# The output projection of a macaron block: as a stage of its own, or as the end of the last head's part

## The reference

```python
x = x + 0.5 * ffn(layernorm(x))          # 512 -> 4096 (gate, up) -> 512, 4-bit weights
x = x + attention(layernorm(x))          # 16 heads of 32, causal, softmax, then w_out and b_out
x = x + 0.5 * ffn(layernorm(x))
```

## Time and profile before

| what | value |
|---|---|
| median of three runs | 3092.0 us |
| the profiled execution | 3097.03 us |
| its span, first to last instruction | 3095.2 us |
| PE busy in the span | 2950.5 us (95%) |
| DVE busy | 1850.3 us (60%) |
| ACT busy | 1061.2 us (34%) |
| POOL busy | 759.4 us (25%) |
| mean granted PE clock | 0.978 |

### The profile page before, as it was taken

One profiled execution on the slowest core, in us unless ns is written; L12 is line 12 of the kernel. 1 busy time (PEld: TensorE's weight loads), 2 busy tenths in 40 slices (PEclk: granted clock), 3 DMA queues, 4 the chain that ended last, 5 costly groups with the idle time before them and its releaser, 6 DMA issues. The chain is left out here.

```text
span 3095.2 us, 38971 instructions
## 1 busy us (share of the span) xinstructions
PE 2950.5 (95%) x13152; PEld 2210.6 (71%) x13152; DVE 1850.3 (60%) x3290; ACT 1061.2 (34%) x1797; POOL 759.4 (25%) x481
## 2 busy tenths in 40 slices
PE   5999999999999989999999996679999999999999
PEld 3788888888888858654454453458888888888887
DVE  7666655665655564666666661476655666556554
ACT  4322222222222232365565564142222222222222
POOL 4322222222222235300000001343222222222221
PEclk9999999999999989999999998789999999999999
DMA  3000000000000027622222221201000000000001
GB/s 95 21 28 27 21 27 20 25 22 27 27 20 20 1 58 165 178 56 55 55 55 55 55 53 51 80 7 35 27 22 20 27 27 21 27 20 25 23 14 55
DMA packets 120569, 127.58 MB, mean 41 GB/s; under 512 B 72672, under 2 KB 72928, under 8 KB 117152
## 3 DMA queue, kind: packets, MB, share of 16 engines
q1 hardware_dynamic: 119928, 125.93, 15.5%
q10 hardware_dynamic: 552, 0.59, 0.1%
HBM read 96.87 MB, written 29.62 MB: 41 GB/s over the span
## 5 line engine op out<-in xcount | busy, mean ns | idle before, releaser
L61 PE MATMUL psum<-ffn_x_high,ffn_w_high 128*128 128x512 f32 x2048 | 803.2, 392 | 18.6 <-DVE ffn_gelu L389 18.6
L62 PE MATMUL psum<-ffn_x_low,ffn_w_high 128*128 128x512 f32 x2048 | 798.9, 390 | 0.0
L63 PE MATMUL psum<-ffn_x_high,ffn_w_low 128*128 128x512 f32 x2048 | 798.5, 390 | 0.0
L526 POOL TENSOR_TENSOR ffn_inner<-ffn_gelu,ffn_inner 128x512 fp32r<-128x512 f32 x256 | 346.6, 1354 | 1156.0 <-ACT ffn_inner L471 1156.0
L379 DVE SCALAR_TENSOR_TENSOR ffn_gelu<-ffn_gelu,psum 128x512 f32<-128x512 f32 x256 | 176.1, 688 | 599.2 <-ACT ffn_gelu L464 599.1
L61 PEld LDWEIGHTS psum<-ffn_x_high,ffn_w_high 128*128 128x128 f32 x2048 | 386.0, 188 | 103.9 <-DVE ffn_gelu L389 22.0
L62 PEld LDWEIGHTS psum<-ffn_x_low,ffn_w_high 128*128 128x128 f32 x2048 | 385.9, 188 | 82.1 <-issue 2.0
L63 PEld LDWEIGHTS psum<-ffn_x_high,ffn_w_low 128*128 128x128 f32 x2048 | 385.7, 188 | 80.4
L61 PE MATMUL psum<-ffn_inner,ffn_w_high 128*128 128x512 f32 x1024 | 398.6, 389 | 0.2
L62 PE MATMUL psum<-ffn_inner,ffn_w_high 128*128 128x512 f32 x1024 | 398.4, 389 | 0.0
L63 PE MATMUL psum<-ffn_inner,ffn_w_low 128*128 128x512 f32 x1024 | 398.3, 389 | 0.0
(11 more groups left out here) (114 smaller groups left out, 3168.0 us busy)
## 6 DMA issues: line engine op xcount, KB each, us to landing
ffn_words<-packed SPq DMA_DIRECT2D x96, 256.0 KB
ffn_word_scales<-scales SPq DMA_DIRECT2D x96, 256.0 KB
qk_parts<-parts SPq DMA_DIRECT2D x32, 512.0 KB, 4.0
queries<-qk_parts SPq DMA_DIRECT2D x48, 256.0 KB, 4.1
keys<-qk_parts SPq DMA_DIRECT2D x48, 256.0 KB, 6.1
x<-x_in SPq DMA_DIRECT2D x4, 1024.0 KB, 13.3
v_parts<-parts SPq DMA_DIRECT2D x16, 256.0 KB, 4.6
values<-v_parts SPq DMA_DIRECT2D x16, 256.0 KB, 7.7
```

What stands on the lines that cost most here:

```text
L61: pe.matmul(out, w_high, x_high, start=first, stop=False, skip_group_check=True)
L62: pe.matmul(out, w_high, x_low, start=False, stop=False, skip_group_check=True)
L63: return pe.matmul(out, w_low, x_high, start=False, stop=last, skip_group_check=True)
L526: pool.tensor_tensor(inner[:, tb % 2, m, 1, :], product[m], f32(inner[:, tb % 2, m, 0, :]), ALU.subtract)\
```

## The change

The second block of code is gone. The projection's 16 steps stand in PE's program straight behind the last head's last batch, and the other engines' parts of them stand in the last head's code.

- Steps have a new order (`STEPS`): blocks 2, 3, 1 with k = 0 to 2, then (2,3) and (3,3), then block 0 with k = 0 to 2, then (1,3), (0,3). They lie in a ring of eight units. A step's loads, its product and its low part share one place (`from_heads` and `normed_low` are overlaid), so unit n % 8 is loaded again when PE has used step n - 8.
- Output tiles are accumulated over groups of steps (`LAST_OF_GROUP`), eight in all, in banks 4 to 7 (one group in 0 to 3). DVE adds each group to x, so a tile of x is updated twice: 32 updates where there were 16, the second without the bias.
- DVE inverts the sums of heads 0 to 11 after head 13, not after the last. SP then loads the first eight units and their inverses, before head 14's stores. The sums of heads 12 to 14 follow; ACT's copies of the first eight steps stand one behind each of the last head's first eight batches.
- The last head's values have 32 columns of ones (the tiles of values are 64 wide), so that each block's product carries its sums on 32 partitions. DVE inverts these and multiplies (`last_head_out`), four times, straight into rows 96 to 127 of the units with k = 3. The last head is not stored. The loads of these units have 96 rows.
- The ring of exponentials has 8 places, not 12; `wo_low` is overlaid with `wo`.

```diff
-RING = 3 * BATCH
+RING = 2 * BATCH
...
-        self.values.append(ctx.enter_context(nc.sbuf_tensor(f"values{i}", [P, TT, VCOLS], F32)))
-        if i < 2:
-            ctx.enter_context(nc.sbuf_tensor(f"values_pad{i}", [P, TT, HD], F32))
+        self.values.append(ctx.enter_context(nc.sbuf_tensor(f"values{i}", [P, TT, LANE], F32)))
...
-        engine.memset(self.values[i][:, :, HD:VCOLS], 1.0).then_inc(self.constants_ready, 1)
+        engine.memset(self.values[i][:, :, HD:LANE], 1.0).then_inc(self.constants_ready, 1)
...
+STEPS = [(b, k) for b in (2, 3, 1) for k in range(LATE_K)] + [(2, LATE_K), (3, LATE_K)]
+STEPS += [(0, k) for k in range(LATE_K)] + [(1, LATE_K), (0, LATE_K)]
+UNITS = 8
+LAST_OF_GROUP = [2, 5, 8, 9, 10, 13, 14, 15]
+LAST_HEAD_OUT = (2, 3, 1, 0)
+SCALED = [0, 1, 2, 3, 4, 5, 6, 7, 8, 9, "block 2", 10, 11, 12, "block 3", 13, 14, 15, "block 1", "block 0"]
...
         self.wo_high = sb("wo_high", [P, KT, D], F32R)
+        with ExitStack() as overlaid:
+            self.wo = overlaid.enter_context(nc.sbuf_tensor("wo", [P, KT, D], F32))
         self.wo_low = sb("wo_low", [P, KT, D], F32R)
         self.out_bias = sb("out_bias", [P, KT], F32)
         self.inverse_all = sb("inverse_all", [P, HEADS * TOKENS // P], F32)
-        self.from_heads = sb("from_heads", [P, 2, KT, TB], F32)
-        self.inverse = sb("inverse", [P, 2, KT, TB], F32)
+        with ExitStack() as overlaid:
+            self.from_heads = overlaid.enter_context(nc.sbuf_tensor("from_heads", [P, UNITS, TB], F32))
+        self.normed_low = sb("normed_low", [P, UNITS, TB], F32R)
+        self.normed_high = sb("normed_high", [P, UNITS, TB], F32R)
+        self.inverse = sb("inverse", [P, UNITS, TB], F32)
+        self.last_inverse = sb("last_inverse", [P, TB], F32)
...
+def load_from_heads(queue, o, o_heads, n):
+    b, k = STEPS[n]
+    queue.dma_start(o.from_heads[0:o.rows(n), n % UNITS, :], o_heads[k * P:k * P + o.rows(n), cols(b, TB)])\
+         .then_inc(o.unit_loaded[n % UNITS], 16)
...
-            for tb in range(2):
-                load_from_heads(sp, o, o_heads, tb, slice(0, EARLY), o.early_loaded[tb])
+            for n in range(UNITS):
+                load_from_heads(sp, o, o_heads, n)
             store(HEADS - 4, 1)
-            store(HEADS - 4, 2)
             sp.wait_ge(o.inverse_ready, 1)
             move_sums(sp, o, inverses, EARLY_HEADS, False, o.inverse_stored)
-            store(HEADS - 4, 3, [0, 1])
             sp.wait_ge(o.inverse_stored, 16)
-            for tb in range(2):
-                for k in range(EARLY):
-                    load_inverse(sp, o, inverses, tb, k, o.early_loaded[tb])
-            store(HEADS - 4, 3, [2])
-            wait_for_stores(HEADS)
+            for n in range(UNITS):
+                load_inverse(sp, o, inverses, n)
+            store(HEADS - 4, 2)
+            wait_for_stores(LAST)
+            move_sums(sp, o, sums, LATE_HEADS, True, o.sums_loaded)
+            sp.wait_ge(o.inverse_ready, 2)
+            move_sums(sp, o, inverses, LATE_HEADS, False, o.inverse_stored)
+            sp.wait_ge(o.inverse_stored, 32)
+            for n in range(UNITS, len(STEPS)):
+                sp.wait_ge(o.tile_done, KT * (n - UNITS + 1))
+                load_from_heads(sp, o, o_heads, n)
+                load_inverse(sp, o, inverses, n)
...
+            def project(n):
+                k = STEPS[n][1]
+                g = group_of(n)
+                first = g == 0 and n == 0 or g > 0 and n == LAST_OF_GROUP[g - 1] + 1
+                pe.wait_ge(o.scaled_low, n + 1)
+                if n == 0:
+                    pe.wait_ge(o.wo_low_ready, 1)
+                    pe.wait_ge(heads.max_taken, SLOTS * HEADS)
+                    pe.wait_ge(heads.rows_ready, NTB * HEADS)
+                for f in range(KT):
+                    if first and g >= 1 and g != 6:
+                        pe.wait_ge(o.x_updated, KT * (5 if g == 7 else g - 1) + f + 1)
+                    split_products(pe, bank[f if g == 6 else 4 + f], o.wo_high[:, k, cols(f, P)],
+                                   o.wo_low[:, k, cols(f, P)], o.normed_high[:, n % UNITS, :],
+                                   o.normed_low[:, n % UNITS, :], first, n == LAST_OF_GROUP[g])\
+                        .then_inc(o.tile_done, 1)
...
+                    if t % BATCH == BATCH - 1:
+                        for v in range(t + 1 - BATCH, t + 1):
+                            with_values(hp, 0, v, columns=LANE)
+                for n in range(len(STEPS)):
+                    project(n)
...
+            def last_head_out(b):
+                e = [b in blocks for blocks in OUTS].index(True)
+                n = STEPS.index((b, LATE_K))
+                row = LANE_OF[b] * LANE
+                dve.wait_ge(out_free, 3 * LAST + e + 1 + 3)
+                dve.reciprocal(o.last_inverse[row:row + HD, :], heads_out[row + HD:row + LANE, e // 2, :])\
+                   .then_inc(o.last_inverse_ready, 1)
+                dve.wait_ge(o.last_inverse_ready, LAST_HEAD_OUT.index(b) + 1)
+                dve.tensor_tensor(o.from_heads[P - HD:P, n % UNITS, :], heads_out[row:row + HD, e // 2, :],
+                                  o.last_inverse[row:row + HD, :], ALU.mult).then_inc(o.scaled, 1)
...
+                    if k == LATE_K:
+                        dve.tensor_tensor(tile, product, tile, ALU.add).then_inc(o.x_updated, 1)
+                    else:
+                        dve.scalar_tensor_tensor(out=tile, in0=product, scalar=o.out_bias[:, f:f + 1], in1=tile,
+                                                 op0=ALU.add, op1=ALU.add).then_inc(o.x_updated, 1)
...
+            head(HEADS // 3 - 1, 0)
+            head(HEADS // 3 - 1, 1)
+            invert(EARLY_HEADS, 1)
+            head(HEADS // 3 - 1, 2)
+            for n in range(6):
+                scale(n)
+            invert(LATE_HEADS, 2)
+            scale(6)
+            scale(7)
+            update(0)
+            scale(8)
+            scale(9)
+            last_head_out(2)
+            update(1)
+            scale(10)
+            scale(11)
+            scale(12)
+            last_head_out(3)
+            scale(13)
+            update(2)
+            update(3)
+            scale(14)
+            scale(15)
+            update(4)
+            last_head_out(1)
+            last_head_out(0)
+            update(5)
+            update(6)
+            update(7)
...
+            def high(n):
+                act.wait_ge(o.scaled, scaled_at(n))
+                act.activation(o.normed_high[:, n % UNITS, :], o.from_heads[:, n % UNITS, :], ACT.Copy)\
+                   .then_inc(o.scaled_high, 1)
+            def last_head(hp):
+                for t in range(SLOTS):
+                    if t + AHEAD < SLOTS:
+                        exps(hp, 0, t + AHEAD)
+                    if t in ROWS_AT and ROWS_AT[t] in OWN_ROWS:
+                        heads.store_rows(act, hp, 0, ROWS_AT[t])
+                    if t % BATCH == BATCH - 1:
+                        if t // BATCH < UNITS:
+                            high(t // BATCH)
+                        take_outs(hp, 0, t, columns=LANE)
+                for n in range(UNITS, len(STEPS)):
+                    high(n)
...
```

More of the change, by code:

```diff
@@ L1113, in inverse_tile, with rows, load_inverse @@
         return self.inverse_all[:, first:first + per_row], per_row
[L1116 to L1132, removed]
+    def rows(self, n):
+        return P - HD if STEPS[n][1] == LATE_K else P
+def load_from_heads(queue, o, o_heads, n):
+    b, k = STEPS[n]
+    queue.dma_start(o.from_heads[0:o.rows(n), n % UNITS, :], o_heads[k * P:k * P + o.rows(n), cols(b, TB)])\
+         .then_inc(o.unit_loaded[n % UNITS], 16)
+def load_inverse(queue, o, inverses, n):
+    b, k = STEPS[n]
+    heads = o.rows(n) // HD
+    queue.dma_start(o.inverse[0:o.rows(n), n % UNITS, :],
+                    inverses[k * HPT:k * HPT + heads, cols(b, TB)].unsqueeze(1).broadcast_to([heads, HD, TB]))\
+         .then_inc(o.unit_loaded[n % UNITS], 16)
 def move_sums(queue, o, dram, heads, to_chip, moved):
@@ L1139, in move_sums, with attention @@
     queue.dma_start(tile if to_chip else rows, rows if to_chip else tile).then_inc(moved, 16)
-def attention(nc, bank, o_heads, sums, inverses, w_out, b_out, heads, o):
+def attention(nc, x, bank, o_heads, sums, inverses, w_out, b_out, heads, o):
     with ExitStack() as ctx:
@@ L1248, in with_values @@
                 row = t % 2 * LANE
-                last = pe.matmul(out_bank[row:row + VCOLS, off:TB], values[i][:, kt, :],
+                last = pe.matmul(out_bank[row:row + columns, off:TB], values[i][:, kt, 0:columns],
                                  probs[:, (SLOTS * s + t) % RING, 0:TB - off], start=(t in FIRST_OF_BLOCK),
@@ L1253, in with_values, with masks_of, head @@
                     last.then_inc(out_ready, 1)
-            def head(hp, s, has_next):
+            def masks_of(s, u, in_batch):
```

(28 more changed lines are left out.)

179 lines of the change are left out of this document (49 added, 130 removed).

## The result

The changed kernel takes 3061.06 us (median of 4 runs, 3058.49 to 3062.78) against 3092.08 (4 runs, 3090.91 to 3094.72): 31.0 us less, ratio 0.9898 with the interval [0.9881, 0.9915]. Forecast were 3062 us and 29.8 us less. It was run twice more beside the experiments: 3058.21 against 3092.89 (ratio 0.9886 [0.9871, 0.9901]) and 3058.97 against 3091.48 (0.9892 [0.9876, 0.9909]), 34.7 and 32.5 us less. So the change is worth 31 to 35 us, and the forecast was 1 to 5 us short of that.

The account below looks back on a forecast made before the run. PE was busy 95%, with two holes of 35.0 us together resting on DMA; 1986.67 - 1955.9 = 30.8, less 0.3 and 0.7, gave 29.8 us, so 3092.0 - 29.8 = 3062.2 us; 8-in-10 range 3055 to 3072.

Parts of the forecast that it names:

- The hole is gone: Between last head and projection, 21.4 us without PE work: steps 0 to 7 wait for nothing, PE continues at full clock.
- The early part is hidden: Head 14: DVE's early inversion costs 0, at most 1.35 us; eight spread inverses on SP, together 21.2 us, cost 0.
- The last head, +0.3: Last head: ACT's eight copies fit between batches at 0; PE's wider loads of values cost 0.3 us, bounds 0 and 2.
- rival A: DVE products slower than single prices, in a stretch where POOL worked: 13.6 us at worst, about 6 likely, 3068; chance 0.17.
- The loads of steps 8 to 15: Projection: first load lands at 1911.0, each further unit 3.3 us later, ahead of PE's use.
- DVE as the bound: Projection: DVE works 40.5 us from 1914.4 plus a 1.0 us hole, ending at 1955.9; PE alone 1947.3.
- rival B: Last head's inversions cost 0.84 us each, so PE sets the end, about 1950.8: 3057; chance 0.08.
- The clock: Projection: PE's 2.2 us wait at step 9 could lower its clock, moving the end 1.4 us; half taken, 0.7.
- The rest at 0: Second feed-forward layer begins behind the same meeting of engines with the same loads: 0.
- D: PE's clock stays down through last head and projection, 12.7 us behind before: 3105; chance 0.03.
- E: ACT stands at a copy whose unit isn't there; no gain beyond the barrier, within 6 us of before: 3090; chance 0.03.
- C: Projection loads land late: 4 us more each moves the end 3.7; with 5 us units 15.5 later, 3078; chance 0.07.

Follow-up runs that it names:

- early-part experiment: Kernel before with DVE's loop end unrolled and only the first inversion and its loads moved forward: 3076.79 us against 3092.89.
- loop-end experiment: Kernel before with only DVE's last round of three heads written as straight code: 3089.76 us against 3092.89.
- fully unrolled kernel: Changed kernel with DVE's loop over the heads wholly in straight code: 3048.82 us against 3058.97 for the changed kernel.

## Why the prediction was right, and where it was short

*The hole is gone.* Right, and by the mechanism given. The early-part experiment prices it: 14.4 of 21.4 us were the queue, 7.0 the rest.

*The early part is hidden.* Right: head 14 took 37.50 us between stores instead of 37.04, inside the 0 to 1.35 allowed. SP spent 13.05 us issuing the eight spread loads, in head 14.

*The last head, +0.3.* It was 33.4 us from head 14's last store to its last product, and 34.1 before. ACT's copies fit between its batches, as said. One thing was not foreseen and cost nothing: DVE's first six products took 8.02 us, not 4.1, beside POOL's 4.94 us subtraction for `wo_low`:

```profile
1860.76 8.02 DVE L1366 TENSOR_TENSOR from_heads<-from_heads,inverse 128x512 f32<-128x512 f32 x6
```

That is rival A's mechanism, in a place where nobody waits. In the changed kernel's tail it did not show, as no product there fell beside a subtraction: the products were 0.64 to 0.69 us. The updates did fall beside four of them (POOL from 1923.65 to 1928.66) and kept 0.64 to 0.69. With the inversions moved it did show in two traces, in product 13, at 1.66 and 1.75 us. What the page "SBUF — State Buffer" of the Trainium skill says (section "Who interferes with whom") held in both places: products with two SBUF inputs were slowed (8.02 us for six), updates were not.

*The loads of steps 8 to 15.* The load of step 9 was waited for until 1908.05, 12.5 us behind the stage's start; forecast were 11.8. 3.3 us for each further unit were 3.4 to 3.5. That the rest is ahead of its use held only as long as the inversions took up DVE's time; with these gone, the loads were the next bound. The prediction also contradicts itself here: it calls itself wrong if a load lands after DVE reaches its product from step 10 on, and its own sum has such a hole of 1.0 us at step 12. The trace has 1.33 us there, so the sum was right and that sign was not.

*DVE as the bound.* The inversions took 3.35 and 3.34 us on 32 partitions, so rival B (0.84) is out. The stage took 53.55 us; the forecast had 53.35, 54.05 with the 0.7 for the clock (the 0.3 was for the last head). But the sum hit it partly by luck. PE's waits were 1.25, 2.04 and 0.49 (the last for POOL), 3.8 in all, where 0.6, 2.2, 1.3 and 1.1 were written, and DVE itself waited 0.9 us for a PE at the lower clock. "Without a pause" was nearly, not wholly right. Without the inversions the kernel gains 3.8 us (3058.97 to 3055.22) and, with DVE's loop unrolled, 3.4 (3048.82 to 3045.45), so DVE's lead over the next bound was some 3 to 4 us and not 13.4.

*The clock.* It fell behind the wait at step 9, as was given a half chance, for four microseconds. That half-speed loss is in the 53.55.

*The rest at 0.* Here the forecast was short. It took the attention loop as unchanged, though the diff takes one jump out of DVE's loop. That is 3.1 us by its own experiment, and 30.6 + 3.1 = 33.7 lies within the three measurements (31.0, 32.5 and 34.7). The trace of before had it: DVE's wait of 2.9 us "issue" at each round's beginning, and an interval of 41 us between heads beside 37.

*The chances.* D (the clock stays down), E (ACT stands in the last head) and C (loads late by 4 us or more) did not happen. C was nearer than it looked: the spread loads by four engines are behind both holes of the kernel before, and were the next limit after the change.

## What to carry over

Before joining two stages, look at what is queued ahead of the transfer that the border waits for, and at how that transfer is cut over the DMA engines: a DMA share of 0.26 at 99 GB/s with all engines waiting was worth 19.9 us by itself, and reordering took 14.4 us off the first hole (the two gains overlap in that hole and do not add up). When work moves onto an engine that was idle, write out that engine's own order with its waits: here DVE's list gave the stage to within 1 us, in part by luck, where PE's sum alone (44.8 us) was 8.8 us too low. And a diff that unrolls a round of a loop for convenience has an effect of its own; compare the round's border in the trace with an ordinary border.

## What was not expected of the hardware

A jump of DVE's loop over 120 tiles' code costs 2.8 to 3.1 us of DVE time in every trace, while the same round's end on PE and ACT shows nothing once DVE's is gone. In the 5 us around the fourth border the DMA table of the kernel before lists two packets of the instruction queue, the changed kernel and the loop-end experiment none; over the attention it is 27 packets before, 24 after, and 16 for the fully unrolled kernel. The line for the fourth border of before, and the one for the attention of the unrolled kernel:

```profile
q14 instruction: 2, 0.02, 1.0%
```

```profile
q14 instruction: 16, 0.13, 0.1%
```

So instructions come in at the jump, and the straight code, although longer, brings fewer packets and no such wait. That the fetch is what DVE waits for is argued, not shown: whether a shorter round would jump for nothing wasn't tried. The Trainium skill, "Advanced Engine Details and Errata", has 108 ns for a compare-and-branch ("Control Flow Timing") and, under "ISA Cache", a store of 32 KB of instructions in two lines for an engine and 128 KB for TensorE. The second would fit what is seen, that PE's jump is free and DVE's is not, but how long either round's code is was not measured; the first is far from the 2.9 us measured here.

Of one spread load, 256 KB from four rows: 2.65 us as one transfer at a DMA share of 0.26 and 99 GB/s; as four transfers 0.47 us of SP's time for each, at a share of 0.56 and 144 GB/s. "DMA: Bandwidth & Descriptors" of the Trainium skill, section "Why a DMA increments its semaphore by 16 and not by 1", gives the rule for the number of engines: at most 16, and it has to divide the slowest dimension, which is 4 for the one transfer and 32 for each of the four. The experiment bears it out in so far as the share was a quarter for the one transfer and twice that for the four.

A pause of PE of 2.0 to 2.3 us may or may not bring the clock down: in two traces of the same kernel, a wait of 2.3 us did not, one of 3.5 did, and in the changed kernel one of 2.04 did. In the attention of the kernel before, waits of 2.12, 2.15 and 2.23 us did and one of 2.31 did not, so the length of the wait alone does not decide. The stages of the two traces of one kernel differ by 3.2 us; 1.2 of this is the longer wait itself.
